# Self-attention with a 1x1 convolution on one core: the split keys and queries written to their rows directly, without placing matmuls

## The reference: what is computed

```python
q = einsum('oc,bcn->bon', Wq, xf) + bq      # 32 channels
k = einsum('oc,bcn->bon', Wk, xf) + bk      # 32 channels
v = einsum('oc,bcn->bon', Wv, xf) + bv      # 256 channels
att = softmax(einsum('bdi,bdj->bij', q, k) / sqrt(32))
out = gamma * einsum('bcj,bij->bci', v, att)
fused = einsum('oc,bchw->bohw', Wf, concatenate([out, x])) + bf
```

## Time and profile before

| | us |
|---|---|
| median of 3 runs (2214.52 to 2215.31) | 2214.78 |
| span of the profiled execution, first to last instruction | 2212.5 |
| outside the span, by the median | 2.3 |
| PE busy | 2179.2 (98%), 9808 matmuls |
| DVE busy | 1667.1 (75%) |
| ACT busy | 1663.0 (75%) |
| POOL busy | 1296.2 (59%) |

### The profile page before, as it was taken

How to read it: one execution, slowest core, us unless ns; L and a number is a source line. 1 busy time by engine, 2 the same in 40 slices (tenths; PEclk the granted TensorE clock), 3 DMA queues, 4 the chain that set the end, 5 groups by cost and what they waited for, 6 DMA issues and landing times.

```text
span 2212.5 us, 30655 instructions
## 1 busy us (share of the span) xinstructions
PE 2179.2 (98%) x9808; PEld 1780.7 (80%) x9808; DVE 1667.1 (75%) x2063; ACT 1663.0 (75%) x1860; POOL 1296.2 (59%) x553
## 2 busy tenths in 40 slices
PE   8999999999999999999999999999999999999997
PEld 7888888888878888888787888888878888888886
DVE  5778888785777888887577788888757778888874
ACT  5677777778567777777856777777776777777786
POOL 0366666667136666666713666666670466666666
PEclk9999999999999999999999999999999999999999
DMA  2000000000200000000020000000001000000000
GB/s 92 1 1 10 28 9 9 9 0 10 76 1 1 10 28 9 9 9 0 20 67 2 1 10 28 9 9 9 9 20 58 1 1 10 9 9 9 9 10 19
DMA packets 18703, 35.25 MB, mean 16 GB/s; under 512 B 1488, under 2 KB 2256, under 8 KB 18640
## 3 DMA queue, kind: packets, MB, share of 16 engines
q1 hardware_dynamic: 18368, 34.35, 4.5%
q10 hardware_dynamic: 272, 0.07, 0.0%
HBM read 17.63 MB, written 16.78 MB: 16 GB/s over the span
## 4 chain that ended last, share of the span: by engine, by line
PE 96%; DVE 1%; issue 1%; ACT 1%; POOL 0%; DMA 0%; POOLq 0%; DVEq 0%; ACTq 0%
PE ps_o L421 62%; PE ps_s L373 11%; PE ps_m L268 9%; PE ps_s L261 6%; PE ps_o L261 4%; PE ps_m L305 1%; DVE lo L603 0%; PE ps_m L359 0%; PE ps_m L366 0%; PE ps_m L367 0%; PE ps_s L282 0%; PE ps_s L283 0%; POOL acc L791 0%; ACT probs L531 0%; DVE inv_sum L701 0%
## 5 line engine op out<-in xcount | busy, mean ns | idle before, releaser
L791 POOL TENSOR_TENSOR acc<-acc,probs 128x1024 f32<-128x1024 f32 x448 | 1090.2, 2433 | 580.5 <-ACT probs L531 580.5
L608 DVE TENSOR_REDUCE part_max<-ps_m 128x1 f32<-128x512 f32 (+1 forms) x1024 | 699.2, 687 | 267.2 <-PE ps_m L268 225.0
L528 ACT ACTIVATE hi<-ps_s 128x1024 fp32r<-128x1024 f32 x508 | 522.0, 1027 | 399.7 <-PE ps_s L373 399.7
L421 PE MATMUL ps_o<-hi,val_hi 128*128 128x512 f32 x2048 | 811.1, 396 | 1.5 <-DVE o_raw L726 1.1
L421 PE MATMUL ps_o<-hi,val_lo 128*128 128x512 f32 x2048 | 803.9, 393 | 0.0
L675 DVE TENSOR_TENSOR lo<-ps_s,hi 128x1024 fp32r<-128x1024 f32 x508 | 615.7, 1212 | 188.1 <-ACT ps_s L532 185.5
L421 PE MATMUL ps_o<-lo,val_hi 128*128 128x512 f32 x2048 | 610.2, 395 | 0.0
L532 ACT ACTIVATE ps_s<-ps_s 128x1024 f32<-128x1024 f32 x508 | 524.7, 1033 | 0.0
L531 ACT ACTIVATE probs<-ps_s 128x1024 f32<-128x1024 f32 x508 | 518.3, 1020 | 0.0
L421 PEld LDWEIGHTS ps_o<-hi,val_hi 128*128 128x128 f32 x2048 | 386.3, 189 | 93.5 <-DVE o_raw L726 7.4
L421 PEld LDWEIGHTS ps_o<-lo,val_hi 128*128 128x128 f32 x2048 | 387.7, 189 | 90.8
(11 more groups left out here) (79 smaller groups left out, 1314.3 us busy)
## 6 DMA issues: line engine op xcount, KB each, us to landing
xf<-x SPq DMA_DIRECT2D x32, 512.0 KB, 3.6
out<-conv SPq DMA_DIRECT2D x32, 512.0 KB, 2.8
conv<-wf2T SPq DMA_DIRECT2D x1, 256.0 KB, 4.0
conv<-wv SPq DMA_DIRECT2D x1, 256.0 KB, 4.3
conv<-wf1T SPq DMA_DIRECT2D x1, 256.0 KB, 4.7
conv<-wkqT ACTq DMA_DIRECT2D x1, 64.0 KB, 4.4
vec<-vectors SPq DMA_DIRECT2D x1, 3.0 KB, 4.1
```

Of the source, the lines that this page charges most:

```text
L421: last = nc.tensor.matmul(ps_o[:, c], v[:, 2 * t + h, c * P:(c + 1) * P], p[:, t % 2, h, :], start=(t == 0 and i in (0, len(lead[0]))), st ...
L528: nc.scalar.activation(hi[:, t % 2], banks, ACT.Exp, scale=SCALE).then_inc(p_hi_done, 1)
L608: nc.vector.reduce_max(part_max[:, i, bass.ds(c, 1)], ps_m[:, i % 2], AX_X).then_inc(m_free, 1)
L791: nc.gpsimd.tensor_tensor(acc[:], acc[:], probs[:, t % PB], ALU.add).then_inc(acc_done, 1)
```

## The change

The key and query weights now stand in the order k, k, q, q instead of k, q, k, q, so the product in `ps_s[:, 0]` has the keys on rows 0 to 63 and the queries on rows 64 to 127. ACT writes k_hi straight to rows 0 to 63 of `keys`, and q_hi in two instructions to rows 0 to 31 and 64 to 95 of `queries`. DVE writes k_lo to rows 64 to 95 of `keys` and q_lo to rows 32 to 63 of `queries`. The placing matmuls, their matrices, and the two copies behind them are gone. A bias column `bkkqq` in the new row order is made once. The queries' low part waits until ACT has read the same rows (`q_hi_done`).

```diff
-                def place_kq():
-
-                    pe.wait_ge(kq_split, C + 1)
-                    nc.tensor.matmul(ps_s[0:R3, 0], place_k[:], kq[:], start=True, stop=True).then_inc(k_placed, 1)
-                    nc.tensor.matmul(ps_s[0:R3, 1], place_q[:], kq[:], start=True, stop=True).then_inc(q_placed, 1)
-
...
-                convolve(1, place_kq)
+                convolve(1)
...
                     if j == JC // 2 and before_last(c):
                         pe.wait_ge(x_split, C + 2)
+                        pe.wait_ge(q_out, C + 1)
                         project_kq(1 - p)
...
-            def kq_hi(C):
+            def kq_hi(c, C):
 
                 act.wait_ge(kq_ready, C + 1)
-                nc.scalar.activation(kq[:], ps_s[:, 0], ACT.Identity, bias=bkq).then_inc(kq_hi_done, 1)
+                nc.scalar.activation(keys[0:2 * CK, span(c)], ps_s[0:2 * CK, 0], ACT.Identity,
+                                     bias=bkkqq[0:2 * CK]).then_inc(k_hi_done, 1)
+                for to in (0, 2 * CK):
+                    last = nc.scalar.activation(queries[to:to + CK, span(c)], ps_s[2 * CK:3 * CK, 0], ACT.Identity,
+                                                bias=bkkqq[2 * CK:3 * CK])
+                last.then_inc(q_hi_done, 1)
...
-                def keys_out():
-                    act.wait_ge(k_placed, C + 1)
-                    nc.scalar.activation(keys[0:R3, span(c)], ps_s[0:R3, 0], ACT.Copy).then_inc(k_out, 1)
-
-                def queries_out():
-                    act.wait_ge(q_placed, C + 1)
-                    nc.scalar.activation(queries[0:R3, span(c)], ps_s[0:R3, 1], ACT.Copy).then_inc(q_out, 1)
-
...
-                def kq_lo(C):
-                    dve.wait_ge(kq_hi_done, C + 1)
-                    tail = kq[2 * CK:4 * CK]
-                    nc.vector.scalar_tensor_tensor(tail, ps_s[2 * CK:4 * CK, 0], bkq[2 * CK:4 * CK], tail.bitcast(F32),
-                                                   ALU.add, ALU.subtract).then_inc(kq_split, 1)
+                def kq_lo(c, C):
+                    dve.wait_ge(k_hi_done, C + 1)
+                    nc.vector.scalar_tensor_tensor(keys[2 * CK:R3, span(c)], ps_s[0:CK, 0], bkkqq[0:CK],
+                                                   keys[0:CK, span(c)].bitcast(F32), ALU.add,
+                                                   ALU.subtract).then_inc(k_out, 1)
+                    dve.wait_ge(q_hi_done, C + 1)
+                    nc.vector.scalar_tensor_tensor(queries[CK:2 * CK, span(c)], ps_s[2 * CK:R3, 0], bkkqq[2 * CK:R3],
+                                                   queries[2 * CK:R3, span(c)].bitcast(F32), ALU.add,
+                                                   ALU.subtract).then_inc(q_out, 1)
```

More of the change, by code:

```diff
@@ L103, in attention_conv @@
         wkq_lo = sb("wkq_lo", [P, KT, 4, CK], F32R)
-        kq = sb("kq", [P, W], F32R)
-        place_k = sb("place_k", [P, R3], F32R)
-        place_q = sb("place_q", [P, R3], F32R)
+        bkkqq = sb("bkkqq", [P, 1], F32)
         ident = sb("ident", [P, P], F32R)
@@ L119, in attention_conv @@
         wkq_raw = raw[:, 1536:1536 + KT * 2 * CK].rearrange("p (k n) -> p k n", k=KT)
+        wkq_twice = raw[:, 1536:1536 + KT * 2 * CK].rearrange("p (u c) -> p u c", c=CK).unsqueeze(2).broadcast_to(
+            (P, KT * 2, 2, CK))
         id_raw = raw[:, 1792:1920]
@@ L137, in attention_conv @@
         x_hi_done, x_split = sem("x_hi_done"), sem("x_split")
-        kq_ready, kq_hi_done, kq_split = sem("kq_ready"), sem("kq_hi_done"), sem("kq_split")
-        k_placed, q_placed, k_out, q_out = sem("k_placed"), sem("q_placed"), sem("k_out"), sem("q_out")
+        kq_ready = sem("kq_ready")
+        k_hi_done, q_hi_done, k_out, q_out = sem("k_hi_done"), sem("q_hi_done"), sem("k_out"), sem("q_out")
+        bkq_spread = sem("bkq_spread")
         conv_ready, conv_done = sem("conv_ready"), sem("conv_done")
@@ L309, in project @@
                 if last_chunk:
-                    place_kq()
                     convolve(0, lambda: (max_scores_0(0), max_scores_0(1)))
@@ L443, in _ @@
             act.wait_ge(wkq_loaded, 16)
-            nc.scalar.activation(wkq_hi[:].rearrange("p k (r u) c -> p k r (u c)", r=2),
-                                 wkq_raw.unsqueeze(2).broadcast_to((P, KT, 2, 2 * CK)), ACT.Copy).then_inc(wkq_hi_done, 1)
+            nc.scalar.activation(wkq_hi[:].rearrange("p k (u r) c -> p (k u) r c", r=2), wkq_twice, ACT.Copy).then_inc(wkq_hi_done, 1)
             def split_x(C, p, k, reused):
@@ L469, in project @@
                     act.wait_ge(vec_loaded, 16)
+                    act.wait_ge(bkq_spread, 1)
                 if not last_chunk:
-                    kq_hi(C)
+                    kq_hi(c, C)
                 if isinstance(C, int) and C == 0:
@@ L501, in project @@
                 conv_out(0)
-                if finishing != 0 and not last_chunk:
-                    keys_out()
-                    queries_out()
                 conv_out(1)
@@ L510, in project @@
                     if h == 0 and before_last(c):
-                        kq_hi(C + 1)
+                        kq_hi(c + 1, C + 1)
                 if last_chunk:
@@ L574, in _ @@
             dve.wait_ge(wkq_hi_done, 1)
-            nc.vector.tensor_tensor(wkq_lo[:].rearrange("p k (r u) c -> p k r (u c)", r=2),
-                                    wkq_raw.unsqueeze(2).broadcast_to((P, KT, 2, 2 * CK)),
-                                    wkq_hi[:].bitcast(F32).rearrange("p k (r u) c -> p k r (u c)", r=2),
-                                    ALU.subtract).then_inc(wkq_split, 1)
+            nc.vector.tensor_tensor(wkq_lo[:].rearrange("p k (u r) c -> p (k u) r c", r=2), wkq_twice,
+                                    wkq_hi[:].bitcast(F32).rearrange("p k (u r) c -> p (k u) r c", r=2), ALU.subtract).then_inc(wkq_split, 1)
             def setup_constants():
@@ L582, in setup_constants, with spread_bkq @@
                 nc.vector.tensor_copy(ident[:], id_raw)
-                for g, (from_k, from_q) in enumerate([(0, 1), (0, 3), (2, 1)]):
-                    s = slice(g * CK, (g + 1) * CK)
-                    nc.vector.tensor_copy(place_k[:, s], id_raw[:, from_k * CK:(from_k + 1) * CK])
-                    nc.vector.tensor_copy(place_q[:, s], id_raw[:, from_q * CK:(from_q + 1) * CK])
+            def spread_bkq():
+                dve.wait_ge(vec_loaded, 16)
+                for g, u in enumerate((0, 0, 1, 1)):
+                    last = nc.vector.tensor_copy(bkkqq[g * CK:(g + 1) * CK], bkq[u * CK:(u + 1) * CK])
+                last.then_inc(bkq_spread, 1)
             def setup_wf2():
@@ L640, in project @@
                     setup_constants()
+                    spread_bkq()
                 if finishing == 0:
@@ L643, in project @@
                     split_acc(b * CHUNKS)
-                kq_lo(C)
+                kq_lo(c, C)
                 if isinstance(C, int) and C == 0:
@@ L662, in project @@
                 if before_last(c):
-                    kq_lo(C + 1)
+                    kq_lo(c + 1, C + 1)
                 chunk_max(b * CHUNKS, 2, c)
```

3 lines of the change are left out of this document (removed).

## The result

The changed kernel takes 2218.18 us (median of 11 runs, 2217.18 to 2220.01) against 2214.55 for the kernel before (11 runs of the same job). The ratio is 1.0018 with a 95% interval of 1.0009 to 1.0026: 3.6 us slower where I had forecast 4.2 faster, and outside my range. The profiled execution has a span of 2215.6 us, 3.1 more than before, and took 2217.41 us as a whole: 1.8 lie outside the span, where the forecast had added 2.3. Kernels timed in rounds have 4 to 10 runs each. The 95% interval of such a difference is about 2 us to each side with 10 runs and 3 to 4 with 4 or 5, so a step of under 2 or 3 us between two kernels is read from their traces and not from the medians.

A forecast was written before the change was run, and what follows sets the result against it. PE's stream was taken to bound the kernel (busy 98%). Terms -14.7 - 0.6 + 5.0 + 4.05 + 2.0 = -4.2 us gave span 2208.3, with 2.3 outside 2210.6 us; 8-in-10 range 2204 to 2217.

The forecast's parts named there:

- the price of ACT's new instructions: ACT's three key and query instructions: 2 x 0.58 + 0.69 = 1.85 us until `q_hi_done`, pixels' high part 1.16 later.
- My bounds on this price: ACT's instructions: lower end the copy without bias, 0.10 shorter each; upper end twice the time while both engines read the bank.
- Nothing is lost in these chunks: Chunks outside 0, 1, 6 and 7: pixels' low part 1.16 us later without a PE wait, next chunk 0.46 sooner.
- 0.46 us of cover: Plain chunks: first maximum ends at 589.6, PE's third score matmul wants its bank at 590.06.
- 14.7: PE: 32 chunks lose two placing matmuls each at 0.23 us, 32 x 0.46 = 14.7 us saved.
- The ten stalls: PE waits: 1.26 us at chunks 6 and 7 (four times), 1.35 in chunk 1, 0.68 lost in chunk 0 (three each).
- this wait goes too: 0.6: Very first chunk: PE's 0.63 us idle before its first score matmul vanishes, saving 0.6 us.
- DVE's price of 0.76 for 32 rows: DVE's two new instructions in place of one: each taken at the 64-row form's 0.76 us.
- The shared bank: Rival: DVE's k_lo and ACT's query reads in one PSUM bank slow each other, up to 0.76 us; 2224.5 us; 6%.
- the other side: Outcome that the changed kernel is slower, over 2219.2 us, from the shared-bank and clock rivals; given 0.07.
- The clock: Rival: new PE stalls of 1.26 and 1.35 us halve the granted clock, 18 us on top, 2228.8 us; 4%.
- Full gain: Rival: DVE catches up, so the stalls at the ten places don't come; 2199.5 us; 10%.

The follow-up runs named there:

- Experiments 2 and 3: Kernel before plus extra ACT instructions after its last work: same rows within a group, 0.57 to 0.59 us apart with bias; then alternating row ranges, 0.70 where start rows change.
- experiment 4: Changed kernel with ACT's three key and query instructions all starting at row 0, some values wrong: 2209.76 us, ratio 0.9977 to before.
- experiment 5: Changed kernel with DVE's k_lo waiting until ACT has done all its key and query reads, so both never read the bank together: 2247.87 us, one run.
- experiment 1: Kernel before without its placing matmuls, ACT copying the unplaced product rows itself (wrong values): 2202.09 us, 12.0 less than before, ratio 0.9947.
- experiment 8: Changed kernel with reciprocals and pixels' low part moved behind first maxima in chunk 0, reciprocals in chunk 1, images 1 to 3: 2213.92 us, ratio 1.0000 to before.
- experiment 9: Changed kernel with pixels ahead of queries in all but first chunks, chunk 7's q_lo behind two maxima, chunks 0 and 1 reordered: 2202.56 us, ratio 0.9948 to before.
- experiment 10: Changed kernel with all lists reordered and chunk 7's q_lo also moved behind chunk 7's maxima into DVE's gap: 2198.29 us, ratio 0.9925 to before.
- experiments 7: Changed kernel with chunk 7's q_lo moved behind the third and fourth maximum of chunk 6: 2217.23 us, ratio 1.0013 to before.

## Why the prediction was wrong

**The step that failed** is the price of ACT's new instructions: "An ACT instruction with a bias delays the next by 0.58 us. I take that for each". The rows of before show 0.58 between two instructions that both start at row 0. The new ones start at row 0, then 64 to 0, then 64 to 64, then pixels at 0, and each step changes a start row. Experiments 2 and 3 put the price of that at 0.12 to 0.13 each, experiment 4 removes it inside the kernel, and the time comes out at 2209.76 against my 2210.6. That is not only the number: in its trace the projection stages of images 1 to 3 are 0.3 to 0.7 us shorter than before where my sum had 0.39, and that of image 0 is 2.9 shorter for my 3.0. My bounds on this price were 0.48 and twice the time by a shared bank: I had looked at the length, the bias and the bank, and not at where the rows begin.

**Plain chunks: "Nothing is lost in these chunks".** I had 0.46 us of cover left when the first maximum was done. The delay came out larger by more than that: 3 x 0.12 = 0.37 from ACT; 0.11 since the first maximum starts 0.03 behind the pixels' low part where I had let it overlap by 0.08; and 0.09 since in the loop ACT starts on the keys 1.68 behind the product's first matmul where the earlier trace rows had 1.59. That is 0.57 against 0.46, thus a wait of 0.11 by these terms, and 0.05 more pass between the maximum's end (591.11) and the matmul, which I had at nothing. Measured are 0.17, and about 0.1 more behind it, for after a waited matmul the next one starts 0.34 later and not 0.24. So each of 16 loop chunks gives 0.26 to 0.30 less than it could.

**The ledger.** By milestones of the two traces, each projection stage of images 1 to 3 became 1.5 to 1.8 us longer, where my sum has 0.39 shorter. Of the 2.07 us between them, 0.9 are the four loop chunks (8.16 on the mean for my 7.93), 0.47 is chunk 7 (1.72 for 1.26), 0.43 chunk 1 (9.72 for 9.29 from its start to the next one's) and 0.20 chunk 0 (its loss grew by 0.87 for my 0.68), 2.0 in all. Image 0 became 0.7 shorter for my 3.0: 1.0 in the loop chunks, 0.5 in chunk 7, and 0.9 at the start, where TensorE came to full speed later than in the execution of before. The eight matmuls that merge the weights, first before, then in the changed kernel:

```profile
10.53 2.06 PE L247 MATMUL ps_o<-conv 128*128 128x256 f32 x8
```

```profile
10.48 2.92 PE L249 MATMUL ps_o<-conv 128*128 128x256 f32 x8
```

In the first they start 0.22 us apart from the second on, in the second row five steps are 0.40 to 0.43 before it is 0.22. PE doesn't idle between them, and the 512-column matmuls just ahead start 0.42 to 0.43 apart in both kernels, as they do at a granted clock of 0.50 in experiment 5. In the twelve traces the closer spacing begins between 10.5 and 13.1 us, whatever the kernel. The attention stages together came out 1.2 shorter, nearly all in image 1, whose stretch of granted clock 0.50 lasted 3.4 us for 6.8. That makes 3 x 2.07 + 2.3 - 1.2 = 7.3 us, which is the whole distance between -4.2 and +3.1. Two of these terms, the 0.9 at the start and the -1.2, are chance of the executions, and they nearly cancel.

**The gain, "14.7".** Right in size: experiment 1 got 12.0 with some stalls left in it, and the loop chunk without waits is 8.39 - 7.88 = 0.51 shorter for my 0.46.

**The ten stalls.** Place and cause right, each too small: 1.26, 1.35 and 0.68 became 1.72, 1.74 and 0.87. Where ACT's spacing is 0.58 they are 1.45, 1.35 and 0.60 (1.05 less the 0.45 of before), so chunks 1 and 0 were priced right. In chunk 7 my 1.26 was for the second of the two score matmuls; with the spacing at 0.58 it is 1.36 late, and the one behind it another 0.10, which I missed.

**The first chunk, "this wait goes too: 0.6".** The wait did go. In the profiled execution of the changed kernel the later clock ate it (12.90 us from chunk 0 to chunk 1, 13.39 before). In experiments 8 and 9, which have the same orders there and came to full speed early, the chunk takes 11.91 and 11.98, so the term was right.

**DVE's price of 0.76 for 32 rows.** Measured 742 and 746 ns; right. By the Trainium skill (VectorE: DVE Perf Modes, section on the TRN2 errata) the estimate would have been 0.66; the measurement decides.

**The rivals.** The shared bank: refuted by experiment 5. Its time, 2224.5, missed by 6.3 us where the forecast missed by 7.6, so by the number alone the wrong reason looked the better one. I gave the other side 7% and thought only of expensive mechanisms for it, though the cover was thin enough for 0.1 us per instruction to tip it. The clock: not reached by these waits of up to 1.6 us. Behind the first chunk the changed kernel's trace has a granted clock of 0.50 in two places only, for 3.4 us at the start of image 1's attention and in the last 10 us. The wait at the attention's start in image 1 was followed by a shorter stretch of lower clock than in the earlier trace rows, that of image 2 again by none, which is part of the -1.2. Full gain: not what this change does, but what experiment 10 reaches.

## What to carry to other kernels

A cover as thin as 0.46 us behind five instructions has to be tested against an error of 0.1 us in each instruction ahead of it, not only against large mishaps. A price taken from one pair of neighbours holds for neighbours of that kind: on ACT keep the start row the same from one instruction to the next, or count 0.13 us for each change. When instructions multiply ahead of something that PE needs, move first what PE needs (here the pixels and the maxima) and put the rest where the engine waits anyway; moving one of them alone only hands the wait on, as experiments 7 and 8 show.

## What was not expected of the hardware

- ACT loses its overlap with the instruction before when the start row of input or output changes: 0.70 against 0.57 us with bias, 0.62 against 0.48 without (512 columns out of PSUM, start rows 0 and 64). The number of rows, the bank, and whether input and output rows are the same make no difference.
- Waits of PE around 2 us may be followed by half the clock. In experiment 5, eight of the ten waits of 1.86 to 2.05 us in the projection stages were, for 3.4 us each, and two, of 1.94 and 1.87 us, were not, while waits of 1.93 and 1.86 at the same places of image 2 were. What decides it stays open. In the changed kernel, behind waits of up to 1.6 us, it wasn't seen, and behind those of 2.4 and 2.7 us at the start of the attention once and once not. An attention stage of image 1 or 2, whose instructions are the same in all these kernels, took 475.0 us without such a stretch, 476.6 with one of 3.4 us and 477.9 with one of 6.8; that is chance of this size in every difference above.
- A DVE subtraction of 1024 columns and a GpSimd addition of the same size, both with two inputs in SBUF, do not run side by side: the one that starts second is about as much longer as the first still lasts. DVE's took 2.74 us for 1.23 in experiment 8, GpSimd's 3.45 for 2.40 in experiment 9, in all three images alike. So moving such an instruction can cost more than it saves, or nothing, by which of the two comes first.
